# The last stage's first expert product taken as three products of rounded parts

## The reference, cut to what matters

```python
def _ffn(h, w1, b1, w2, b2):
    return jax.nn.gelu(h @ w1 + b1, approximate=False) @ w2 + b2

def _seq_moe(h, gw, gb, w1, b1, w2, b2):
    cw = _combine_weights(h.mean(axis=1) @ gw + gb)
    for e in range(E):
        out = out + _ffn(h, w1[e], b1[e], w2[e], b2[e]) * cw[:, e, None, None]
```

## Time and profile before

| | |
|---|---|
| median of three runs | 1320.65 us (1312.6 to 1324.02) |
| the profiled execution, span from first to last instruction | 1327.3 us (no other time of that execution is given) |
| PE busy | 1215.2 us, 92% |
| DVE, ACT, POOL busy | 70%, 61%, 54% |
| last stage, first of its first products to the last instruction | 1186.2 to 1327.3 us of the span |
| in it, from sequence to sequence | 8.0 us |
| chain that ended last | PE 66%, DVE 13%, issue 5%, SP's queue 5% |

### The profile page before, as it was taken

One profiled execution on the slowest core, in us unless ns is written; L12 is line 12 of the kernel. 1 busy time (PEld: TensorE's weight loads), 2 busy tenths in 40 slices (PEclk: granted clock), 3 DMA queues, 4 the chain that ended last, 5 costly groups with the idle time before them and its releaser, 6 DMA issues.

```text
span 1327.3 us, 30592 instructions
## 1 busy us (share of the span) xinstructions
PE 1215.2 (92%) x9884; PEld 990.1 (75%) x9884; DVE 926.7 (70%) x2791; ACT 803.1 (61%) x1629; POOL 710.5 (54%) x1279
## 2 busy tenths in 40 slices
PE   4999999998887699999999899999999999989996
PEld 3777777766665477777777799898677777769996
DVE  6799999988777779989985221125788888635553
ACT  4566666775665366666666556564666666654552
POOL 4455555664231156777778431332677775445654
PEclk9899999998898799999998899999899999979998
DMA  4788776425666354555442787786565565255773
GB/s 118 218 230 239 221 225 185 125 71 155 167 168 163 94 141 127 128 131 136 120 118 63 225 231 232 229 254 209 140 154 146 152 155 148 79 156 166 213 201 103
DMA packets 208291, 216.94 MB, mean 163 GB/s; under 512 B 46403, under 2 KB 157507, under 8 KB 208132
## 3 DMA queue, kind: packets, MB, share of 16 engines
q1 hardware_dynamic: 191088, 193.49, 54.0%
q0 software_dynamic: 6304, 14.43, 3.9%
q10 hardware_dynamic: 10740, 7.06, 1.7%
HBM read 126.90 MB, written 85.46 MB: 160 GB/s over the span
## 4 chain that ended last, share of the span: by engine, by line
PE 66%; DVE 13%; issue 5%; SPq 5%; ACT 4%; DMA 4%; POOL 3%; POOLq 0%; DVEq 0%; ACTq 0%
PE scores L619 6%; PE weights L1573 6%; PE values L709 5%; PE weights L673 5%; PE scores L1831 4%; PE weights L678 4%; PE weights L1847 4%; PE values L716 3%; PE scores L1557 3%; PE scores L628 3%; DVE negmax L1014 3%; SPq L475 3%; DMA windows<-parts 2%; PE tokens L648 2%; PE tokens L582 2%
## 5 line engine op out<-in xcount | busy, mean ns | idle before, releaser
L1170 POOL TENSOR_SCALAR_AFFINE_SELECT probs<-probs 128x256 f32<-128x256 f32 (+1 forms) x576 | 279.5, 490 | 228.7 <-ACT probs L859 225.4
L859 ACT ACTIVATE probs<-weights 128x512 f32<-128x512 f32 x448 | 264.9, 598 | 120.3 <-PE weights L673 86.8
L1014 DVE TENSOR_REDUCE negmax<-scores 128x4 f32<-128x512 f32 x384 | 261.3, 685 | 86.2 <-PE scores L619 83.2
L619 PE MATMUL scores<-keys,queries 128*128 128x512 f32 (+1 forms) x384 | 186.1, 487 | 6.0 <-issue 1.7
L859 ACT ACTIVATE probs<-weights,keybias 128x512 f32<-128x512 f32 x192 | 131.5, 688 | 64.3 <-PE weights L673 48.0
L673 PE MATMUL weights<-queries,keys 104*128 104x256 f32 x768 | 159.0, 290 | 1.0 <-issue 0.6
L673 PEld LDWEIGHTS weights<-queries,keys 104*128 104x128 f32 x768 | 139.9, 194 | 22.3 <-issue 3.6
L1018 DVE TENSOR_REDUCE negmax<-scores 128x2 f32<-128x512 f32 (+1 forms) x192 | 131.0, 686 | 29.2 <-PE scores L625 19.4
L678 PEld LDWEIGHTS weights<-queries,keys 104*128 104x128 f32 x768 | 114.8, 195 | 10.2
L678 PE MATMUL weights<-queries,keys 104*128 104x128 f32 x768 | 110.2, 268 | 0.0
L709 PE MATMUL values<-probs,v 128*32 128x256 f32 x1536 | 106.6, 396 | 3.5 <-POOL probs L1170 3.5
(11 more groups left out here) (285 smaller groups left out, 2747.1 us busy)
## 6 DMA issues: line engine op xcount, KB each, us to landing
windows<-parts SPq DMA_DIRECT2D x192, 192.0 KB
queries<-windows SPq DMA_DIRECT2D x64, 384.0 KB
hidden_room<-in_m_w SPq DMA_DIRECT2D x78, 256.0 KB, 3.1
out_room<-in_m_w SPq DMA_DIRECT2D x78, 256.0 KB, 3.2
keys<-windows SPq DMA_DIRECT2D x192, 96.0 KB
routed_rows<-zeros SPq DMA_DIRECT2D x64, 256.0 KB, 3.6
windows<-parts SPq DMA_DIRECT2D x64, 120.0 KB
expert_rows<-probs ACTq DMA_DIRECT2D x46, 128.0 KB, 3.1
```

Source lines behind the costliest of these rows:

```text
L619: i = pe.matmul(bank[:], queries[0:rows, s, t * P:(t + 1) * P], keys[0:rows, s::S4, half * P:(half + 1) * P], start=True, stop=True)
L859: act.activation(probs[:, n % RING], weight_banks[n % 2][:], ACT.Exp, scale=SCALE, **bias).then_inc(exp_done.sem, 1)
L1014: i = dve.tensor_reduce(most[:, part, s, :], bank[:].rearrange("p (a k) -> p a k", k=P), AX.X, ALU.max, negate=True)
L1170: pool.affine_select(out=block, in_=block, compare_op=ALU.is_ge, fill=0.0, base=0, pattern=[[0, heads], [1, P]], channel_multiplier=-1).th ...
```

## The change

The first product of the last stage becomes three products in float32r: with w1 = wh + wl and h = hh + hl, where the high parts are rounded to float32r, it adds wh*hh + wh*hl + wl*hh in the same bank of PSUM.

- The parts lie in heads 1 to 10 of the attention's key tiles (`keys_of`), another tile per lane.
- ACT casts w1 of each expert, 128x512, to its high part (`act_weights`, slots -3 and -2). DVE subtracts it from w1 for the low part (`dve_weights`, -2 and -1). DVE makes both parts of h (`dve_src`, -4 and -3, 128x256).
- `pe_hidden` has three matmuls where one stood, and waits for `src_split` and `weights_split` in place of the transfers.
- `sp_weights` is cut in two: the two w1 transfers at slot -7, when the low parts of sequence q-3 are made; w2 and the biases at -5, behind the waits of before. Each half reads the experts' numbers again, so there are four `value_load` per sequence where there were two. The wait on w2 and the biases moves to `pe_out` and `act_hidden`.
- The gate's generators and the fetch begin two slots earlier; cw stays at slot -5.

```diff
--- before.py
+++ after.py
@@ -1720,12 +1720,15 @@
             def transfers(name, lanes_of, per):
                 return LaneSignal([semaphore(f"expert_{name}{n}") for n in range(lanes_of)], one, per)
 
-            fetched, base_loaded, weights_loaded = transfers("fetched", LANES, 1), transfers("base_loaded", LANES, 2), transfers("weights_loaded", LANES, 4 * K2)
+            fetched, base_loaded, weights_loaded = transfers("fetched", LANES, 1), transfers("base_loaded", LANES, 2), transfers("weights_loaded", LANES, 3 * K2)
+            first_loaded = transfers("first_weights_loaded", LANES, K2)
             stored = transfers("stored", 2, 1)
             tok_made, turned, src_ready, logits_ready = (signal(n) for n in ("tok_ready", "transposed", "src_ready", "logits_ready"))
             diff_ready, chosen, halves_ready, weights_ready, spread_ready, cw_ready = (
                 signal(n) for n in ("diff_ready", "chosen", "halves_ready", "weights_ready", "spread_ready", "cw_ready"))
             hidden_ready, gelu_done, y_ready = (signal(n, 2 * K2) for n in ("hidden_ready", "gelu_done", "y_ready"))
+            src_high, src_split, weights_high, weights_split = (signal(n, per) for n, per in (
+                ("src_high", 1), ("src_split", 1), ("weights_high", K2), ("weights_split", K2)))
             base_ready, y_taken, res_ready = signal("base_ready"), signal("y_taken", K2), signal("res_ready")
             first_var, first_rstd, last_var, last_rstd = (signal(n) for n in ("first_var", "first_rstd", "last_var", "last_rstd"))
 
@@ -1740,6 +1743,9 @@
             kept = W[:].rearrange("p w t -> p (w t)").bitcast(F32)
             x_kept = [kept[:, n * NT * C:(n + 1) * NT * C].rearrange("p (n c) -> p n c", n=NT) for n in range(LANES)]
             x2_kept, base = [K[n][:, 0:1, :].bitcast(F32).rearrange("p h (n c) -> p (h n) c", n=NT) for n in range(LANES)], base_sum
+            keys_of = [K[(n + 1) % LANES] for n in range(LANES)]
+            w_parts = [keys[:, 1:9].rearrange("p h t -> p (h t)").rearrange("p (k e f) -> p k e f", k=2, e=K2) for keys in keys_of]
+            src_parts = [keys[:, 9:11] for keys in keys_of]
             logits, top, index = logits_rows, top_rows, index_rows
 
             values_bank = Bank(OB)
@@ -1779,14 +1785,20 @@
                 if q == 0:
                     sp.wait_ge(combined.sem, combined.at(B - 1))
                 if q >= LANES:
+                    sp.wait_ge(weights_split.sem, weights_split.at(q - LANES, K2))
+                of = lambda d, e, s: d[bass.ds(e, 1)].rearrange(s)
+                for k in range(K2):
+                    e = sp.value_load(index[lane][0:1, k:k + 1], min_val=0, max_val=E - 1)
+                    sp.dma_start(hidden_w[lane][:, k, :], of(ins["m1_w1"], e, "o p f -> p (o f)")).then_inc(first_loaded.sem(q), 16)
+                yield
+                yield
+                if q >= LANES:
                     sp.wait_ge(y_ready.sem, y_ready.at(q - LANES, 2 * K2))
                     sp.wait_ge(base_ready.sem, base_ready.at(q - LANES))
                 for k in range(K2):
                     e = sp.value_load(index[lane][0:1, k:k + 1], min_val=0, max_val=E - 1)
-                    of = lambda d, s: d[bass.ds(e, 1)].rearrange(s)
-                    sp.dma_start(hidden_w[lane][:, k, :], of(ins["m1_w1"], "o p f -> p (o f)")).then_inc(weights_loaded.sem(q), 16)
-                    sp.dma_start(out_w[lane][:, k], of(ins["m1_w2"], "o p c n -> p (o c) n")).then_inc(weights_loaded.sem(q), 16)
-                    sp.dma_start(hidden_b[lane][:, k], of(ins["m1_b1"], "o p c -> p (o c)")).then_inc(weights_loaded.sem(q), 16)
+                    sp.dma_start(out_w[lane][:, k], of(ins["m1_w2"], e, "o p c n -> p (o c) n")).then_inc(weights_loaded.sem(q), 16)
+                    sp.dma_start(hidden_b[lane][:, k], of(ins["m1_b1"], e, "o p c -> p (o c)")).then_inc(weights_loaded.sem(q), 16)
                     sp.dma_start(out_b[lane][:, k], ins["m1_b2"][bass.ds(e, 1)].to_broadcast([P, C])).then_inc(weights_loaded.sem(q), 16)
                 yield
 
@@ -1818,7 +1830,7 @@
 
             def pe_hidden(pe, q):
                 lane = q % LANES
-                pe.wait_ge(weights_loaded.sem(q), weights_loaded.at(q))
+                pe.wait_ge(src_split.sem, src_split.at(q))
                 for r in range(2 * K2):
                     n = hidden_ready.at(q, r)
                     if n == 0:
@@ -1826,10 +1838,14 @@
                     if n >= 3:
                         pe.wait_ge(gelu_done.sem, n - 2)
                     e, half = divmod(r, 2)
+                    if half == 0:
+                        pe.wait_ge(weights_split.sem, weights_split.at(q, e + 1))
                     for k in range(2):
-                        c = 2 * half + k
-                        i = pe.matmul(hidden_banks[n % 3][:, k * T:(k + 1) * T], hidden_w[lane][:, e, c * P:(c + 1) * P], srcT[lane][:],
-                                      start=True, stop=True)
+                        into, chunk = hidden_banks[n % 3][:, k * T:(k + 1) * T], slice((2 * half + k) * P, (2 * half + k + 1) * P)
+                        high, low = (w_parts[lane][:, part, e, chunk] for part in range(2))
+                        pe.matmul(into, high, src_parts[lane][:, 0], start=True, stop=False)
+                        pe.matmul(into, high, src_parts[lane][:, 1], start=False, stop=False)
+                        i = pe.matmul(into, low, src_parts[lane][:, 0], start=False, stop=True)
                     i.then_inc(hidden_ready.sem, 1)
                     yield
 
@@ -1842,6 +1858,7 @@
                             pe.wait_ge(y_taken.sem, y_taken.at(q - 1, e + 1))
                         elif e == 0:
                             pe.wait_ge(exp_done.sem, exp_done.at(last, units[last].n))
+                        pe.wait_ge(weights_loaded.sem(q), weights_loaded.at(q))
                         pe.wait_ge(gelu_done.sem, gelu_done.at(q, 2 * e + 2))
                     for c in range(FC):
                         i = pe.matmul(y_banks[e][:, t * C:(t + 1) * C], g_of[lane][:, e, c, t * P:(t + 1) * P], out_w[lane][:, e, c, :],
@@ -1852,7 +1869,7 @@
             def act_gate(act, q):
                 act.wait_ge(turned.sem, turned.at(q))
                 if q >= LANES:
-                    act.wait_ge(hidden_ready.sem, hidden_ready.at(q - LANES, 2 * K2))
+                    act.wait_ge(src_split.sem, src_split.at(q - LANES))
                 if q == 0:
                     act.wait_ge(values_projected.sem, values_projected.at(last))
                 if q >= 2:
@@ -1870,6 +1887,7 @@
                     act.wait_ge(pv_done.sem, pv_done.at(last, units[last].groups[-1]))
                 if q >= LANES:
                     act.wait_ge(y_ready.sem, y_ready.at(q - LANES, 2 * K2))
+                act.wait_ge(weights_loaded.sem(q), weights_loaded.at(q))
                 for r in range(2 * K2):
                     n = hidden_ready.at(q, r)
                     e, half = divmod(r, 2)
@@ -1880,6 +1898,41 @@
                                            bias=hidden_b[lane][:, e, c:c + 1])
                     i.then_inc(gelu_done.sem, 1)
                     yield
+
+            def parts_free(engine, q):
+
+                if q < LANES:
+                    before = last - 2 + q
+                    engine.wait_ge(st_ready.sem, st_ready.at(before, units[before].n))
+                else:
+                    engine.wait_ge(hidden_ready.sem, hidden_ready.at(q - LANES, 2 * K2))
+
+            def act_weights(act, q):
+                lane = q % LANES
+                parts_free(act, q)
+                act.wait_ge(first_loaded.sem(q), first_loaded.at(q))
+                for e in range(K2):
+                    act.copy(w_parts[lane][:, 0, e], hidden_w[lane][:, e]).then_inc(weights_high.sem, 1)
+                    yield
+
+            def dve_weights(dve, q):
+                lane = q % LANES
+                for e in range(K2):
+                    dve.wait_ge(weights_high.sem, weights_high.at(q, e + 1))
+                    dve.tensor_tensor(w_parts[lane][:, 1, e], hidden_w[lane][:, e], w_parts[lane][:, 0, e].bitcast(F32),
+                                      ALU.subtract).then_inc(weights_split.sem, 1)
+                    yield
+
+            def dve_src(dve, q):
+                lane = q % LANES
+                parts_free(dve, q)
+                dve.wait_ge(src_ready.sem, src_ready.at(q))
+                dve.tensor_copy(src_parts[lane][:, 0], srcT[lane][:]).then_inc(src_high.sem, 1)
+                yield
+                dve.wait_ge(src_high.sem, src_high.at(q))
+                dve.tensor_tensor(src_parts[lane][:, 1], srcT[lane][:], src_parts[lane][:, 0].bitcast(F32),
+                                  ALU.subtract).then_inc(src_split.sem, 1)
+                yield
 
             def norm_stats(dve, which, z):
                 stats, meanvar, vareps, rstd = norms[which]
@@ -1935,7 +1988,7 @@
```

(12 more changed lines are left out.)

## The result

The changed kernel takes 1352.37 us (median of four runs, 1348.92 to 1352.51) against 1317.76 us for the kernel before (1320.65 until a fourth run of 1314.87 joined the three): a ratio of 1.0245, 95% interval 1.0204 to 1.0286. Run again beside other kernels it takes 1349.89 us against 1321.3, a ratio of 1.0213, 1.0158 to 1.0268. The forecast was 1335 us with a range of 1319 to 1350.

What follows compares the result with a forecast made beforehand. The prediction took PE's own work, 8.02 us per cycle of the last stage, as the bound. New waits on DVE, 24.8 us, less 10.4 saved by faster products gave +14.4 on 1320.65: 1335 us, range 1319 to 1350.

Steps and rivals of the forecast that it cites:

- main step: Last stage: PE waits for DVE's subtraction, queued behind PE's own gate logits; 1.94 us per sequence, 24.8 us in all.
- the clock: Last stage: PE's new gaps might lower the granted clock; left out of the sum, held as a rival at 0.20.
- the start: Sequence 0's gate moves two slots towards the attention's last maxima; nothing put on it, 1 us kept each way.
- The chain PE, DVE, PE: Last stage: logits, DVE's gate step, statistics and subtraction, then PE; 1.94 us for sequences 1 to 12, 1.56 for 13.
- The saving: First product, last stage: three float32r MATMULs replace one float32 product; 0.62 us per sequence, 10.4 us in all.
- the 0.109: The skill's gap for 256 columns, 109 ns; would make the forecast 3.8 us lower; the pair in the trace shows 0.12.
- The forecast's range: 1335 give or take 5, 1319 to 1350 for 8 in 10; a float32r pace of 0.107 gives 3 us back.
- rival A: Last stage: the clock falls too; six short stretches add 10 us, 1345 us, or 22 us, 1357 us; chance 0.20.
- SP: Last stage: two more readings make SP's work 8.6 us per cycle, above 8.02 but covered by the 9.34 us cycle.
- Rival B: Last stage: DVE's chain does not bite, SP's 8.6 us cycles decide; at most +7.0, 1321 to 1328 us; chance 0.13.

Runs made afterwards that it cites:

- e5: Changed kernel with w1's low-part subtraction at rank 3, two readings per sequence, first three sequences' gates, fetches and w1 transfers at old slots: 1313.95 us, ratio 0.9935.
- e2: Changed kernel with the rank of DVE's subtraction for the low parts of w1 altered from 5 to 3: 1339.07 us, ratio 1.011.
- e3: Changed kernel with w1's low-part subtraction at rank 3 and two readings of experts' numbers per sequence instead of four: 1317.87 us, ratio 0.9966.
- e4: Changed kernel with twelve float32r filler products on PE before the wait for w1's low parts, each sequence but the first: 1345.4 us, ratio 1.0158.
- e8: Kernel before with only gates and fetches moved two slots earlier, cw at its slot: 1327.18 us, ratio 1.0047; its profiled execution was disturbed.
- e10: Kernel before with only gates and fetches moved two slots earlier, repeated for an undisturbed profile: 1326.4 us, ratio 1.0033.
- e7: Changed kernel with only the first three sequences' gates, fetches and w1 transfers back at the slots of the kernel before: 1347.2 us, ratio 1.0175.
- e9: Changed kernel with the first three sequences' gates, fetches and w1 transfers at old slots and twelve filler products for sequences 1 to 13: 1340.87 us, ratio 1.0156.
- e11: Changed kernel with w1's low-part subtraction at rank 3, first three sequences' gates, fetches and w1 transfers at old slots, four readings: 1331.39 us, ratio 1.008.
- e6: Changed kernel, unaltered, run once more beside other kernels: 1349.89 us, ratio 1.0213.

## Why the prediction was wrong

Its main step was right, in place and in size; two terms were missing beside it, the clock, which was left out of the sum, and the start, on which it put nothing.

- *The chain PE, DVE, PE.* Forecast 1.94 us for each of sequences 1 to 12 and 1.56 for 13, measured 9.30 - 7.44 = 1.86 between the changed kernel and e5, and 8.91 - 7.44 = 1.47 for 13. e2, e3 and e5 take it away by one rank. Shown, but for sequence 1, whose round trip ends at the attention's last output, 2.2 to 2.9 us, and stays in e5 with 1.5.
- *The saving.* Forecast 0.62 us per sequence, measured 8.02 - 7.44 = 0.58. The pace of the three matmuls is 0.12, as the earlier trace rows had it. The Trainium skill, TensorE: Matmul & The Clock Gate (Back-to-back issue gap), gives the formula behind the 0.109 that the forecast weighed against it for an isolated matmul, not for a stream in which each matmul has its own weight load, as here. The forecast's range had a slip of size in it: at 0.107 the 384 matmuls would give 4.6 to 5 us back, not 3.
- *The clock* was the step that failed: I left it out of the sum and gave it 0.20, as rival A. It came in six cycles of the profile, 1.57 us each, 9.4 us (rival A: six, 1.7 each, 10 us). e4 shows that the gaps bring it: with PE at work in them, clock 1.00 and no cycle over 9.26 but one of 9.71 near the end. My reason against it, that PE is dense between the gaps, did not count: the falls came right behind stretches with one gap of 1.83 us in them and 7 us of dense work ahead of it. The Trainium skill, TensorE: Matmul & The Clock Gate (HAM oscillation), describes recurring waits for transfers, of 3 to 5 us, that throttle the array each time. Here shorter gaps did it, but not each time: six of twelve in one execution and five of twelve in the other brought a fall behind the first y. Why one gap does and the next does not is not shown.
- *The start.* "I put nothing on it, and keep 1 us each way" was the other missing term: 4.4 us by the profiles, 6 us by e8 and e10, from the gates moved two slots earlier, with which more of the end of the attention runs at half clock. Shown by e10 (the loss in a kernel with nothing else changed); the profiles of e7 and e5 show it the other way, though e7's time is not clear of the noise. e9's 23.8 us say that such a stretch also comes at times with the gates in the old place.
- *SP.* 8.6 us per cycle was right (8.70 in e11), and that it would be covered by the longer cycle too. Rival B's condition, no chain, is e11: the queue costs 17 us there against e5, one fall of the clock included, and 11 us against the kernel before, where B had counted 7.0 at most. SP's later steps are longer than its plain sum, up to 10.2 us; what holds them up was not separated.

Put together, from the first y to the last, against e5's 107.0 us (these pieces are read from the same traces, so the sum shows that nothing is left over, no more): eleven waits of 1.86 and one of 1.47 (a cycle of 8.91) are 21.9, six falls of 1.57 are 9.4, and 107.0 + 21.9 + 9.4 = 138.3, the changed kernel's first profile. The kernel before has none of the two, but slower products: 9.0 us more, 116.0. With 2.3 and 4.4 at the start the mean of the profiles is 28.3 of the measured 28.6 us. The forecast of 14.4 lacks 9.4 for the clock and 4.4 for the start.

## What to carry to other kernels

Before moving operand work to another engine, write down what stands ahead of it in that engine's fixed order in the same slot: an instruction that waits for the consumer's own last result turns a covered wait into a round trip, and one rank takes it away. Where a change makes gaps on TensorE, price the clock as a term of the sum and not as a rival, and compare the stretch of the trace before the gap with one that already fell. And count what a queue's owner does besides issuing: two readings of a number per sequence cost 17 us here (e11 against e5), once the larger wait was gone.

## What the hardware showed beyond the expected

In the three profiles with the changed kernel's cycles (the result, e6, e7), each of the 17 falls of the clock behind the first y lasts for 3.4 us though PE is busy all through it, and the cycle with it is 10.86 to 10.89 us instead of 9.29 to 9.32. Filling a gap with useless matmuls gave time back: with twelve of them in each gap the cycle was 9.25 us, 0.05 shorter than a cycle at full clock without them. The kernel's median fell by 4.5 to 7 us with them, and its interval overlaps with that of the kernel without.
